# A gated cross-attention block on one core: the order of two tensor-engine tasks and the end of each step, first attention

## The chip, the core and the metric

The kernel runs on one core of a Trainium2 chip. The engines work in parallel, each through its own instruction queue in program order: PE (matrix products and transposes, into the eight banks of PSUM), ACT (activation functions and copies), DVE (vector operations, reductions), POOL (slow vector operations) and SP (issues the DMAs). They meet only at semaphores. The metric is the device time of one execution in microseconds (us).

## The reference, cut to what matters

Input `x` has 8 batches of 256 tokens with 256 features, the context has 77 tokens per batch. Four blocks follow each other, each added to `x` through a tanh gate:

1. cross-attention with 16 heads of 16 (this is the "first attention", and the only part that the change touches),
2. a sparse feed-forward block with three top-k choices,
3. a second cross-attention with rotary positions and a mask,
4. a mixture of 16 experts with a shared expert.

```python
q = split_heads(x0 @ Wq.T + bq)          # x0 = layernorm(x)
k = split_heads(ctx @ Wk.T + bk)
v = split_heads(ctx @ Wv.T + bv)
attn = softmax(-SCALE * einsum('bhqd,bhkd->bhqk', q, k))
out = einsum('bhqk,bhkd->bhqd', attn, v)
x = x + tanh(g) * (out @ Wp.T + bp)
x = x + tanh(g2) * ffn(layernorm(x))      # needs the second layernorm
```

## The kernel before, in words

The first attention works one batch of 256 queries per step n = 0 to 7. Batches are pipelined: in step n the kernel finishes the attention of batch n, prepares the queries and the softmax maxima of batch m = n + 2, transposes the normalised tokens of batch n + 3, projects the output of batch n - 1 and transposes the second-layernorm tokens of batch n - 2. The order on every engine is written out by hand: `attend` of PE (L1019), `attend` of ACT (L670), `attend_first` of DVE (L1570), `attend` of POOL (L514) and of SP (L380).

The tasks of PE in a step, with the short names used below:

- **KS01, KS23, KS45, KS67** (`key_scores`, L985): scores, keys by queries, of head pairs 0 to 7. Each pair goes to PSUM bank 0 or 1 in turn, so pair p waits until ACT has taken the exponential of pair p - 2 (`exp_done`).
- **PQ** (`project_q(m)`, L919): the query projection of batch m; waits for the copy of its transposed tokens (`xt_done`).
- **FR and SR** (`first_rows(m)`, `second_rows(m)`, L964 and L972): scores queries by keys for the first and second 128 queries of batch m, from which DVE takes the maximum over keys (`maxima`, L1531). Both use the same three banks, so SR waits for the maxima of FR. FR needs the rounded queries of ACT (`high_queries`, L621, "qhi").
- **W0 and W1** (`weigh_values(n, c)`, L1002): probabilities times values and the denominators, for heads 0 to 7 and 8 to 15; they wait for exponentials 3 and 7 of the batch.
- **PO** (`project_out(n-1)`, L935): the output projection; waits for the low part of the queries of m (`low_queries`, L1506, "qlo") because they share a bank.
- **MR** (`maxima_to_rows(m)`, L976): turns the maxima of batch m into rows; ACT copies them out (`maxima_out`, L643), and SP sends them through DRAM into the query operand of step m.
- **TX** (`transpose_xn(n+3)`, L911) and **TS** (`transpose_second(n-2)`, L915): four 128x128 transposes each; ACT copies them out with `copy_xt` (L609) and `round_xt` (L616).

Before the change a step of PE is KS01, PQ, KS23, FR, KS45, PO, SR, W0, KS67, TX, TS, MR, W1. In the steps 6 and 7 there is no batch m any more, and PQ, FR, SR and MR fall away; TX ends with step 4, and TS begins with step 2. All PE instructions of helper `mm` are recorded at L902, the transposes at L908.

ACT's step is: `invert(n-1, 1)` (L660: logarithm and exponential that make 1/denominator once W1 is done), exponentials 0 and 1, qhi, exponentials 2 to 5, `invert(n, 0)` once W0 is done, exponentials 6 and 7, `copy_xt`, `round_xt`, `maxima_out`. DVE's step is in the diff below, with `divide` (L1542) for the division, `add_projection` (L1493), the two parts of the second layernorm, and `low_part` (L1487), which waits for `round_xt`. POOL's step is `inv_std(n+4)` (L472: the 1/sigma that `normalise(n+4)` waits for), the block keys `kbr` of batch n + 3 (L489), the bias and the second 1/sigma. Before step 0 a prologue prepares the batches 0 and 1 completely; SP's `pair_maxima(1)` is its last DMA.

Of the kernel before, what the change touches and what calls it, by code (L numbers as in the profile page):

```python
# [50 lines left out]
def flamingo_kernel(nc, x_d, ctx_d, gates_d, mask_d, maskT_d, const_d,  # L51
                    ropeA_d, ropeB_d, attn_d, pat_d, piw_d,
                    pv_d, oiw_d, op_d, gate_d, wg_d, wu_d, wd_d, sg_d, su_d, sd_d, out_d):
    with ExitStack() as ctx:
# [549 lines left out]
        def _(act):  # L604
# [44 lines left out]
            def exponentials(n, pairs):  # L649
                for p in pairs:  # L650
                    act.wait_ge(score_ps, PAIRS * n + p + 1)
                    if n > 0:
                        act.wait_ge(pv_ps, 2 * n - 1 + p // 4)
                    if n == 0 and p == 0:
                        act.wait_ge(kone_in, 64)
                    act.activation(PT[n // B][0:SK, 2 * p:2 * p + 2, :],  # L656
                                   ps[0:SK, p % 2, :].rearrange("p (e q) -> p e q", e=2), ACT.Exp,
                                   scale=-0.25 if n < B else 1.0).then_inc(exp_done, 1)
# [11 lines left out]
            def attend(layer):  # L670
                lo, hi = B * layer, B * layer + B
                for n in range(lo, hi):
                    if n > lo:
                        invert(n - 1, 1)
                    exponentials(n, (0, 1))
                    if n == 2 * B - 1:
                        round_shared(0)
                    if n + 2 < hi:
                        if layer == 0:
                            high_queries(n + 2)  # L680
                        else:
                            raw_queries(n + 2)
                    exponentials(n, (2, 3, 4, 5))
                    if n == 2 * B - 1:
                        round_shared(1)
                    if n + 2 < hi and layer == 1:
                        high_queries(n + 2)
                    invert(n, 0)
                    exponentials(n, (6, 7))
                    if n + 3 < hi:  # L690
                        copy_xt(n + 3)
                    if n - 2 >= lo and layer == 0:
                        round_xt(n - 2, R_BANK + 1)
                    if n + 2 < hi:
                        maxima_out(n + 2)
                    if n == 2 * B - 1:
                        round_shared(2)
# [202 lines left out]
        def _(pe):  # L900
# [28 lines left out]
            def swap_pairs(m):  # L929
                pe.wait_ge(q_raw, m - B + 1)  # L930
                for g in range(2):
                    ins = mm(ps[:, m_bank(m), S * g:S * g + S], perm, qraw[:, g, :])
                ins.then_inc(q_perm, 1)
# [30 lines left out]
            def first_rows(m):  # L964
                pe.wait_ge(qhi_done, 2 * m + 2)
                pe.wait_ge(kbr_done, m + 1)
                if m > 0:
                    pe.wait_ge(max_done, 2 * m)
                pe.wait_ge(xt_done, m + 1)
                row_scores(m, 0)  # L970

            def second_rows(m):  # L972
                pe.wait_ge(max_done, 2 * m + 1)
                row_scores(m, 1)

            def maxima_to_rows(m):  # L976
                pe.wait_ge(max_done, 2 * m + 2)
                pe.wait_ge(qlo_done, m + 1)
                if m % B >= 3:
                    pe.wait_ge(x_done, m - 2)  # L980
                for t in range(2):
                    ins = mm(ps[0:H, m_bank(m), P * t:P * t + P], mcol[m % 2][:, t, :], ident_r)
                ins.then_inc(mT_ps, 1)

            def key_scores(n, pairs):  # L985
                for p in pairs:
                    if p == 0:
                        pe.wait_ge(k_in[n % 2], 32 * (n // 2 + 1))
                        pe.wait_ge(q_in[n % 2], 16 * (n // 2 + 1))
                        pe.wait_ge(m_in[n % 2], 16 * (n // 2 + 1))  # L990
                    if PAIRS * n + p > 1:
                        pe.wait_ge(exp_done, PAIRS * n + p - 1)
                    out = ps[0:SK, p % 2, :]
                    if n >= B:
                        mm(out.rearrange("p (e q) -> p e q", e=2), ident_b[:, 0:SK],
                           maskTb.unsqueeze(1).to_broadcast([P, 2, S]), True, False)
                    for e in range(2):
                        ins = mm(out[:, S * e:S * e + S], kpair[n % 2][0:KROWS, e, p, :], qpair[n % 2][0:KROWS, p, :],
                                 n < B, True)
                    ins.then_inc(score_ps, 1)  # L1000
# [18 lines left out]
            def attend(layer):  # L1019
                lo, hi = B * layer, B * layer + B  # L1020
                for n in range(lo, hi):
                    m = n + 2
                    key_scores(n, (0, 1))
                    if m < hi:
                        project_q(m)
                    key_scores(n, (2, 3))
                    if m < hi:
                        if layer == 0:
                            if m >= 5:
                                pe.wait_ge(xlo_done, m - 4)  # L1030
                            first_rows(m)
                        else:
                            swap_pairs(m)
                    key_scores(n, (4, 5))
                    if n > lo:
                        project_out(n - 1)
                    if m < hi:
                        if layer == 0:
                            second_rows(m)
                        else:  # L1040
                            first_rows(m)
                    weigh_values(n, 0)
                    if m < hi and layer == 1:
                        second_rows(m)
                    key_scores(n, (6, 7))
                    if n + 3 < hi:
                        pe.wait_ge(max_done, 2 * n + 6)
                        transpose_xn(n + 3)
                    if n - 2 >= lo and layer == 0:
                        if m < hi:  # L1050
                            pe.wait_ge(max_done, 2 * n + 6)
                        else:
                            pe.wait_ge(xlo_done, n - 2)
                        transpose_second(n - 2, R_BANK + 1, xn2[:, n % 2])
                    if m < hi:
                        maxima_to_rows(m)
                    weigh_values(n, 1)

            def project_keys(layer, j):
                g, nh = divmod(j, 2)  # L1060
# [371 lines left out]
        def _(dve):  # L1432
# [98 lines left out]
            def maxima(m, t):  # L1531
                dve.wait_ge(row_ps, 2 * m + t + 1)
                if m >= 2:
                    dve.wait_ge(mT_ps, m - 1)
                op = ALU.min if m < B else ALU.max
                heads = mcol[m % 2][:, t, :].rearrange("p (g h) -> p g h", g=2)
                dve.tensor_reduce(heads[:, :, 0:6], ps[:, R_BANK:R_BANK + 2, 0:6 * SK].rearrange("p g (h k) -> p g h k", k=SK),  # L1537
                                  AX, op, negate=True)
                dve.tensor_reduce(heads[:, :, 6:8], ps[:, R_BANK + 2, 0:4 * SK].rearrange("p (g h k) -> p g h k", g=2, k=SK),  # L1539
                                  AX, op, negate=True).then_inc(max_done, 1)  # L1540
# [29 lines left out]
            def attend_first():  # L1570
                for n in range(B):
                    if n > 0:
                        divide(n - 1, 1)
                    if n + 4 < B:
                        stats(n + 4)
                    if n + 2 < B:
                        low_queries(n + 2)
                    if n + 2 < B:
                        maxima(n + 2, 0)
                    if n + 4 < B:  # L1580
                        normalise(n + 4)
                    if n > 0:
                        add_projection(n - 1)
                    if n + 2 < B:
                        maxima(n + 2, 1)
                    if n > 0:
                        stats_second(n - 1)
                    if n == B - 1:
                        dve.wait_ge(kbr_done, B)
                        dve.wait_ge(xt_ps, B)  # L1590
                        for s in range(2):
                            split_patterns(0, s, None)
                    divide(n, 0)
                    if n > 0:
                        normalise_second(n - 1)
                    if n >= 2:
                        low_part(n - 2, R_BANK + 1)
# [454 lines left out]
```

## Time and profile before

| what | us |
|---|---|
| median of 3 runs | 807.88 (806.72 to 808.96) |
| profiled execution, its own time | 805.65 |
| its span in the trace | 803.8 |
| PE busy in the span | 693.6 (86%) |
| DVE, ACT, POOL busy | 453.2, 334.9, 219.9 |

The page of the profile gives the busy time of each engine, and the chain that ended last (73% of it on PE, 13% on DVE, 5% on ACT). The first attention with its steps 0 to 7 lies between about 35 and 148 us of the span. To read it, take the timeline of one step, put every row to its task by its operands (`ps<-keep,att` is PQ, `ps<-att,big` PO, `ps<-kbr,qhi` FR or SR, `ps<-qpair,kpair` key scores, `ps<-big,vp` the start of W0 or W1), and ask at each start what ended last before it. Starts are compared with starts: the rows of consecutive matmuls overlap.

### The profile page before, as it was taken

To read this page: it belongs to the slowest core of one execution; us is meant where nothing else is said; L and a number is where in the kernel's file an instruction comes from. 1 tells how busy PE (TensorE), PEld (TensorE's weight loads), DVE (VectorE), ACT (ScalarE), POOL (GpSimd) and SP (SyncE) were. 2 spreads that over 40 slices of the span, in tenths; PEclk is the share of its full clock that TensorE was granted. 3 is DMA by queue.
4 is the path that set the end of the run, shared out by engine and by line. 5 is a ranking of instruction groups with operands and counts; after the bars stand their busy time and mean duration, and the time that the engine had idled before them with its cause. 6 is when DMAs were issued, how large, how long until landed. Compare 5 with 4: busy or idle time off the path is not lost.

```text
span 803.8 us, 13689 instructions
## 1 busy us (share of the span) xinstructions
PE 693.6 (86%) x5104; PEld 556.7 (69%) x5104; DVE 453.2 (56%) x919; ACT 334.9 (42%) x757; POOL 219.9 (27%) x200
## 2 busy tenths in 40 slices
PE   5789998989996745766799998899988899999998
PEld 4556665668884423444566665699976799999997
DVE  4447773411006565747566563655878778788712
ACT  3245655556661110021355446423227655655510
POOL 6433421100000310024535521100005544554400
PEclk9869998999998865997899999999999999999999
DMA  6664672192000053004353342400000356566313
GB/s 241 179 169 134 173 207 74 66 403 84 11 0 2 1 199 96 8 0 123 88 134 94 98 127 54 154 5 1 1 1 1 108 198 219 193 195 233 127 37 105
DMA packets 61478, 87.22 MB, mean 109 GB/s; under 512 B 17264, under 2 KB 50800, under 8 KB 60400
## 3 DMA queue, kind: packets, MB, share of 16 engines
q1 hardware_dynamic: 61424, 86.49, 33.9%
q8 instruction: 35, 0.57, 0.3%
q14 instruction: 19, 0.16, 0.1%
HBM read 63.54 MB, written 18.73 MB: 102 GB/s over the span
## 4 chain that ended last, share of the span: by engine, by line
PE 73%; DVE 13%; issue 5%; ACT 5%; DMA 4%; SPq 1%; POOL 0%; ACTq 0%; DVEq 0%; POOLq 0%
PE ps L902 70%; DVE keep L1719 2%; PE ps L908 1%; DVE keep L1730 1%; ACT big L656 1%; DMA keep<-in_gates 1%; ACT keep L666 1%; DMA keep<-in_x 1%; DVE keep L1712 1%; DVE keep L1727 1%; PE ps L1379 1%; DMA k_rows<-klo 1%; DMA m_rows<-big 1%; DVE mcol L1539 1%; DVE mcol L1537 1%
## 5 line engine op out<-in xcount | busy, mean ns | idle before, releaser
L902 PE MATMUL ps<-keep 128*128 128x120 bf16 (+9 forms) x517 | 83.5, 286 | 38.7 <-DVE keep L1719 30.7
L902 PEld LDWEIGHTS ps<-keep 128*128 128x128 bf16 (+2 forms) x517 | 42.2, 119 | 65.7 <-DVE keep L1719 43.7
L902 PE MATMUL ps<-thi,whi 128*128 128x256 f32 x256 | 73.7, 288 | 4.3 <-POOL tlo L591 2.1
L902 PE MATMUL ps<-thi,wlo 128*128 128x256 f32 x256 | 72.4, 283 | 0.0
L902 PE MATMUL ps<-tlo,whi 128*128 128x256 f32 x256 | 72.4, 283 | 0.0
L745 ACT ACTIVATE ps<-ps 128x256 f32<-128x256 f32 x128 | 47.6, 372 | 38.6 <-PE ps L902 38.6
L902 PE MATMUL ps<-qpair,kpair 98*77 98x256 f32 x256 | 60.7, 355 | 3.3 <-ACT big L656 2.0
L495 POOL TENSOR_TENSOR kbr<-khi,keep 128x616 fp32r<-128x616 f32 x32 | 41.4, 1316 | 63.4 <-PE ps L902 63.4
L815 ACT ACTIVATE att<-ps 128x512 f32<-128x512 f32 x48 | 28.6, 596 | 68.6 <-PE ps L902 68.0
L902 PEld LDWEIGHTS ps<-thi,whi 128*128 128x128 f32 x256 | 49.0, 191 | 6.3 <-issue 4.1
L902 PE MATMUL ps<-xhi,phi 128*128 128x512 f32 x128 | 50.7, 396 | 2.9 <-ACT ps L745 2.9
L902 PE MATMUL ps<-big,vp 77*32 77x256 f32 (+1 forms) x384 | 46.8, 404 | 4.2 <-ACT big L656 3.9
L902 PE MATMUL ps<-xhi,plo 128*128 128x512 f32 x128 | 50.3, 393 | 0.0
L902 PE MATMUL ps<-xlo,phi 128*128 128x512 f32 x128 | 50.1, 392 | 0.0
L902 PEld LDWEIGHTS ps<-qpair,kpair 98*77 98x77 f32 x256 | 35.8, 157 | 20.0 <-issue 9.2
L902 PEld LDWEIGHTS ps<-tlo,whi 128*128 128x128 f32 x256 | 49.1, 192 | 0.0
L902 PEld LDWEIGHTS ps<-thi,wlo 128*128 128x128 f32 x256 | 49.0, 192 | 0.0
L666 ACT ACTIVATE keep<-ps,keep 128x256 f32<-128x256 f32 x32 | 15.2, 475 | 78.9 <-PE ps L902 78.9
L1855 DVE TENSOR_TENSOR att<-att,ps 128x512 f32<-128x512 f32 x48 | 32.7, 681 | 26.3 <-ACT att L815 23.5
L902 PE MATMUL ps<-kbr,qhi 128*128 128x154 f32 (+1 forms) x128 | 37.5, 404 | 9.7 <-DVE mcol L1539 4.1
L902 PE MATMUL ps<-big,keep 77*32 77x256 f32 (+3 forms) x480 | 40.8, 422 | 3.4 <-DVE keep L1809 1.0
L902 PE MATMUL ps<-keep,att 128*128 128x256 f32 x128 | 37.1, 442 | 4.5 <-ACT keep L613 4.5
(219 smaller groups left out, 1813.1 us busy)
## 6 DMA issues: line engine op xcount, KB each, us to landing
qpair<-q_rows SPq DMA_DIRECT2D x16, 768.0 KB, 5.6
q_rows<-qhi SPq DMA_DIRECT2D x32, 256.0 KB, 2.7
big<-in_piw SPq DMA_DIRECT2D x4, 2048.0 KB, 12.4
q_rows<-qlo SPq DMA_DIRECT2D x16, 256.0 KB, 2.9
att<-in_wg SPq DMA_DIRECT2D x8, 512.0 KB, 3.7
att<-in_wu SPq DMA_DIRECT2D x8, 512.0 KB, 4.7
att<-in_wd SPq DMA_DIRECT2D x8, 512.0 KB, 5.4
big<-in_wg SPq DMA_DIRECT2D x8, 512.0 KB, 3.6
```

The costliest lines, as they stand in the source:

```text
L495: ins = pool.tensor_tensor(kbr[n % 2][:, g], words(khi)[:, g, SK * b:SK * b + SK].unsqueeze(1).to_broadcast([P, HG, SK]), hmask.unsqueeze( ...
L656: act.activation(PT[n // B][0:SK, 2 * p:2 * p + 2, :], ps[0:SK, p % 2, :].rearrange("p (e q) -> p e q", e=2), ACT.Exp, scale=-0.25 if n < ...
L666: act.activation(r, ps[:, PV_BANK + c, S:2 * S], ACT.Ln, bias=tiny[:, 0:1]).then_inc(ln_done, 1)
L745: ins = act.activation(part, part, ACT.Gelu, accum_out=acts[:, bass.ds(ch * 8 + (2 * g + h), 1)])
L815: act.activation(hgl[:, f, :], ps[:, 2 * f, :], ACT.Gelu).then_inc(gelu_done, 1)
L902: return pe.matmul(out, lhsT, rhs, start=start, stop=stop, skip_group_check=True)
L908: ins = pe.transpose(ps[:, bank, at:at + P], src[:, t, P * c:P * c + P], ident)
L1379: ins = pe.transpose(ps[:, c_at + g // 2, at:at + P], GW[b % 2][:, t, P * g:P * g + P], ident)
L1537: dve.tensor_reduce(heads[:, :, 0:6], ps[:, R_BANK:R_BANK + 2, 0:6 * SK].rearrange("p g (h k) -> p g h k", k=SK), AX, op, negate=True)
L1539: dve.tensor_reduce(heads[:, :, 6:8], ps[:, R_BANK + 2, 0:4 * SK].rearrange("p (g h k) -> p g h k", g=2, k=SK), AX, op, negate=True).then_ ...
L1719: dve.tensor_tensor(reached[:, lo:hi, 8:P].rearrange("p c (j b) -> p c j b", b=8), chunked(keys)[:, lo:hi, :].unsqueeze(2) .to_broadcast([ ...
L1855: dve.tensor_tensor(hval, hgl[:, f, :], ps[:, 2 * f + 1, :], ALU.mult).then_inc(hval_done, 1)
```

## The change

For the first attention alone (layer 0): on PE, FR goes from between KS23 and KS45 to behind PO, and SR from in front of W0 to behind it; W1 goes from the end of the step to directly behind KS67; MR follows W1 and stands ahead of TX and TS. On ACT, `maxima_out` goes ahead of `copy_xt` and `round_xt`. On DVE, the first maxima go behind `normalise(n+4)` and `add_projection(n-1)`, and the second behind `divide(n, 0)`. So PE's new step is KS01, PQ, KS23, KS45, PO, FR, W0, SR, KS67, W1, MR, TX, TS. No instruction is added or removed; the second attention keeps its order.

```diff
--- before.py
+++ after.py
@@ -687,11 +687,13 @@
                         high_queries(n + 2)
                     invert(n, 0)
                     exponentials(n, (6, 7))
+                    if n + 2 < hi and layer == 0:
+                        maxima_out(n + 2)
                     if n + 3 < hi:
                         copy_xt(n + 3)
                     if n - 2 >= lo and layer == 0:
                         round_xt(n - 2, R_BANK + 1)
-                    if n + 2 < hi:
+                    if n + 2 < hi and layer == 1:
                         maxima_out(n + 2)
                     if n == 2 * B - 1:
                         round_shared(2)
@@ -1024,25 +1026,23 @@
                     if m < hi:
                         project_q(m)
                     key_scores(n, (2, 3))
-                    if m < hi:
-                        if layer == 0:
-                            if m >= 5:
-                                pe.wait_ge(xlo_done, m - 4)
-                            first_rows(m)
-                        else:
-                            swap_pairs(m)
+                    if m < hi and layer == 1:
+                        swap_pairs(m)
                     key_scores(n, (4, 5))
                     if n > lo:
                         project_out(n - 1)
                     if m < hi:
-                        if layer == 0:
-                            second_rows(m)
-                        else:
-                            first_rows(m)
+                        if layer == 0 and m >= 5:
+                            pe.wait_ge(xlo_done, m - 4)
+                        first_rows(m)
                     weigh_values(n, 0)
-                    if m < hi and layer == 1:
+                    if m < hi:
                         second_rows(m)
                     key_scores(n, (6, 7))
+                    if layer == 0:
+                        weigh_values(n, 1)
+                        if m < hi:
+                            maxima_to_rows(m)
                     if n + 3 < hi:
                         pe.wait_ge(max_done, 2 * n + 6)
                         transpose_xn(n + 3)
@@ -1052,9 +1052,10 @@
                         else:
                             pe.wait_ge(xlo_done, n - 2)
                         transpose_second(n - 2, R_BANK + 1, xn2[:, n % 2])
-                    if m < hi:
-                        maxima_to_rows(m)
-                    weigh_values(n, 1)
+                    if layer == 1:
+                        if m < hi:
+                            maxima_to_rows(m)
+                        weigh_values(n, 1)
 
             def project_keys(layer, j):
                 g, nh = divmod(j, 2)
@@ -1575,14 +1576,12 @@
                         stats(n + 4)
                     if n + 2 < B:
                         low_queries(n + 2)
-                    if n + 2 < B:
-                        maxima(n + 2, 0)
                     if n + 4 < B:
                         normalise(n + 4)
                     if n > 0:
                         add_projection(n - 1)
                     if n + 2 < B:
-                        maxima(n + 2, 1)
+                        maxima(n + 2, 0)
                     if n > 0:
                         stats_second(n - 1)
                     if n == B - 1:
@@ -1591,6 +1590,8 @@
                         for s in range(2):
                             split_patterns(0, s, None)
                     divide(n, 0)
+                    if n + 2 < B:
+                        maxima(n + 2, 1)
                     if n > 0:
                         normalise_second(n - 1)
                     if n >= 2:
```

## Rows read from the trace of the kernel before

**Rows 1.** The chain that ended last, shares by line, first attention (43 to 148 us).

```profile
by line: PE ps L902 75.6%; ACT big L656 8.3%; issue 7.8%; ACT keep L666 4.6%; ACT qhi L628 1.0%; PE ps L908 0.8%; ACT keep L668 0.6%; DVE mcol L1539 0.5%; DVE qlo L1510 0.5%; DVE big L1546 0.4%; ACTq L653 0.2%; ACTq L626 0.1%; ACTq L612 0.1
```

**Rows 2.** Busy time by stretch: us, then PE, PEld, DVE, ACT, POOL, clock, DMA share, GB/s.

```profile
80.00:92.90 12.90, 12.13 (x117) 8.91 (x116) 10.22 (x28) 7.78 (x18) 5.38 (x7) 1.00 0.67 188
...
118.90:131.30 12.40, 10.41 (x92) 6.50 (x92) 5.12 (x14) 6.80 (x15) 2.85 (x5) 0.86 0.58 162
```

**Rows 3.** The chain that ended last in order of time: start, us, what.

```profile
93.54 4.76 PE ps L902 x48
...
98.30 0.59 issue
...
106.47 4.75 PE ps L902 x48
```

**Rows 4.** Timeline from W1 of batch 3 to W1 of batch 4: start, us, what.

```profile
93.38 0.59 ACT L613 ACTIVATE keep<-ps 128x512 f32<-128x512 f32 x1
...
93.86 0.59 ACT L618 ACTIVATE xhi<-ps 128x512 fp32r<-128x512 f32 x1
...
94.34 0.36 ACT L647 ACTIVATE big<-ps 16x256 f32<-16x256 f32 x1
...
95.40 0.70 PE L902 MATMUL ps<-qpair,kpair 98*77 98x256 f32 x4
...
95.54 0.47 ACT L666 ACTIVATE keep<-ps,keep 128x256 f32<-128x256 f32 x1 [0.85 <-PE ps L902]
...
96.37 1.06 ACT L656 ACTIVATE big<-ps 77x512 f32<-77x512 f32 x2
...
97.48 0.82 PE L902 MATMUL ps<-qpair,kpair 98*77 98x256 f32 x4
...
97.95 0.84 ACT L628 ACTIVATE qhi<-ps,att 128x256 fp32r<-128x256 f32 x2 [0.52 <-PE ps L902]
...
98.68 1.07 ACT L656 ACTIVATE big<-ps 77x512 f32<-77x512 f32 x2
...
99.57 0.69 PE L902 MATMUL ps<-qpair,kpair 98*77 98x256 f32 x4
...
100.10 1.89 PE L902 MATMUL ps<-att,big 128*128 128x256 f32 x8
...
102.53 1.07 PE L902 MATMUL ps<-big,vp 77*32 77x256 f32 x16
...
104.53 0.47 ACT L666 ACTIVATE keep<-ps,keep 128x256 f32<-128x256 f32 x1 [3.45 <-PE ps L902]
...
104.93 0.60 PE L908 MATMUL ps<-keep 128*128 128x128 f32 x4
...
105.36 1.06 ACT L656 ACTIVATE big<-ps 77x512 f32<-77x512 f32 x2
...
105.36 0.60 PE L908 MATMUL ps<-keep,big 128*128 128x128 f32 x4
...
105.72 0.36 PE L902 MATMUL ps<-ident_r,mcol 128*16 128x128 f32 x2
```

**Rows 5.** Timeline: POOL's block keys and DVE's second normalisation side by side.

```profile
94.31 2.46 POOL L495 TENSOR_TENSOR kbr<-khi,keep 128x616 fp32r<-128x616 f32 x2
...
94.38 2.54 DVE L1484 TENSOR_SCALAR big<-keep 128x256 f32<-128x256 f32 x2 [0.76 <-POOL keep L487]
```

**Rows 6.** The large reduction of the maxima: name, count, ns min/median/max, starts.

```profile
L1537 DVE TENSOR_REDUCE mcol<-ps x32: 1085/1120/1121, 23.3 to 481.3; 128x12 fp32r<-128x924 f32 x32
```

**Rows 7.** Timeline of batches 0 and 1.

```profile
44.50 1.03 PE L902 MATMUL ps<-kbr,qhi 128*128 128x462 f32 x4 [1.77 <-DVE mcol L1539]
...
50.07 0.23 SPq L364 DMA_DIRECT2D qpair<-m_rows  x1
...
54.73 1.14 PE L902 MATMUL ps<-qpair,kpair 98*77 98x256 f32 x4
```

**Rows 8.** Busy time by stretch, one microsecond of W1 to projection of batch 1.

```profile
54.00:55.00 1.00, 1.00 (x9) 0.27 (x2) 0.00 (x0) 0.13 (x1) 0.00 (x0) 0.50 0.63 134
```

## The prediction

> **What bounds the kernel now.** Four views in this order. The chain by line, cut to the first attention, says who ends last there: PE for three quarters, then ACT with exponentials (L656) and the inversions (L666), and 7.8% "issue" [rows 1]. So this stage is a PE queue with ACT links in it. The busy time by stretch says how tight: 12.13 of 12.90 us in a full step, 10.41 of 12.40 in step 6, at a mean clock of 0.86 [rows 2]. PE can give back at most some 0.8 us per full step. The chain in time gives the period: W1 of batch 3 starts at 93.54, that of batch 4 at 106.47, so 12.93 us; inside is one stop of 0.59, where FR waits for qhi [rows 3]. The timeline of that step gives the distances that the new order has to be laid out with [rows 4]; zero is the start of W1(n), 93.54:
>
> - KS01 at +1.86 (so W1, and W0 too, holds PE 1.86); ACT's inversion at +2.00, after 0.85 idle; exponential 0 0.83 behind it, at +2.83.
> - qhi at +4.41, just when PQ ends; exponential 2 at +5.14, 3 done at +6.21.
> - PO at +6.56, W0 2.43 later (8.99), its inversion 2.00 behind W0, exponentials 6 and 7 from 2.83 to 3.90, W1 again at +12.93.
> - TX to TS 0.43, TS to MR 0.36, both behind KS67, while ACT inverts and takes exponentials 6 and 7 [rows 4]. PE would have to wait for exponential 7 anyway: this work is covered and costs nothing now. Likewise `copy_xt`, `round_xt`, `maxima_out` (0.48 from start to start, the last 0.36 long) lie on ACT under W1, where it has nothing else to do.
>
> **The change part by part.**
>
> *1. TX, TS and MR behind W1.* The cover is gone on PE: between W1 and the next KS01 and PQ now lie MR (two products; between 0.1 and 0.36, I take 0.25, somewhat under its row), TX 0.43 and TS 0.36: together 1.04. PQ ends at 4.41 + 1.04 = 5.45.
>
> *2. ACT's three copies.* They now wait for PE: `maxima_out` from +2.22 (1.86 + 0.36), `copy_xt` when TX is done, 1.86 + 0.25 + 0.60 = +2.71, `round_xt` behind it at +3.19, or with TS's end at 3.14. Queued behind them on ACT are the inversion of W1, exponentials 0 and 1 and qhi, which KS23, FR and all of DVE's query work wait for. The inversion starts at +3.67 and not +2.00, exponential 0 at 4.50, exponential 1 ends at 5.57. qhi starts at about 5.47: both roads, PE's and ACT's, arrive together, 1.06 late. Between the ends "ACT alone is late" (1.67, less the 0.5 it was early at qhi) and "PE alone" (1.04) hardly anything is open.
>
> *3. FR away from in front of KS45.* The 0.59 wait goes, but what is late next stands right behind: KS45 needs exponentials 2 and 3, which come behind qhi on ACT. They end at 5.47 + 0.73 + 1.07 = 7.27. So PE, free after KS23 at about 5.9, waits for them about 1.3 us in two pieces where it waited 0.59 and worked on FR. PO starts 0.35 behind exponential 3 (as now: 99.75 to 100.10), at 7.62: 1.06 late. Gain of this edit: none.
>
> *4. FR in SR's place, SR behind W0.* From PO to W0 one row-score task as before: 2.43, W0 at 10.05. Behind it PE has SR (about 0.6) and KS67. Pair 6 is scored 1.86 + 0.6 + 0.5 = 3.0 after W0, where the inversion lets ACT go on at 2.83: 0.15 lost. W1 starts at 10.05 + 3.0 + 1.07 + 0.04 = +14.16. The period is 14.16 against 12.93: **1.2 us more in each full step**. MR's maxima are no stop: SR's are done some 2 us after SR, W1 takes 1.86, and they must be ready only behind it.
>
> *5. DVE.* The first maxima now wait for `normalise(n+4)`, which falls together with POOL's block keys (both start when `inv_std` is done). DVE's two normalisations beside the block keys (two operations, 2.46) took 2.54 [rows 5], where others take 0.4 each. Unhindered, the maxima (1.12 and 0.47 [rows 6]) are ready before W0 ends; held up, they end about 0.3 late for SR. That is 0 to 0.6 per step in steps 2 and 3, the only full ones with a normalisation; I take 0.3. The Trainium skill, page "SBUF — State Buffer", section "SBUF: two separate sides", says that POOL and a DVE operation in a two-port mode exclude each other for a whole instruction, while operands in PSUM stay outside. By it the old order was a good cover (maxima read PSUM) and the new one a bad one; by the plain mean of the unhindered rows the 0.3 would be 0.
>
> *6. Step 0.* SR waits 1.77 us there for maxima and starts at 44.50; the clock then falls to 0.50 [rows 7, 8]. In the new order KS45, FR and W0 fill that time (to about 45.0), but the maxima come behind `normalise(4)` under the block keys: 2.4 later, so SR at 46.9, KS67, exponentials to 49.0, W1 at 49.05. At half clock W1 takes 3.7, MR and TX 1.4: KS01(1) at 54.15 against 54.73 [rows 7], a gain of 0.6. Bounds: if the clock holds, 51.6; but KS01(1) needs the maxima's DMA, issued at 50.07 [rows 7] and some 2 us on its way, so 52.1 at the best: 3 gained. The other way, 0.5 lost.
>
> *7. Steps 6, 7 and the way out.* No PQ, so ACT's late inversion counts in full. Behind W1(5): MR, TS, `maxima_out`, `round_xt` before the inversion, which starts 1.3 late; behind W1(6) and W1(7): TS and `round_xt`, 0.36 + 0.25 to its end + 0.48, about 1.0 late each, and the feed-forward block starts behind the last. Bounds 0.6 and 1.4 each.
>
> *8. SP.* `maxima_out` comes 1.5 to 2 us later, so `pair_maxima` too, with the queries of n + 3 behind it. The result is wanted a whole period later; I cost it nothing (0 to 0.2 a step).
>
> **The sum.** Step 0: -0.6. Step 2 (no TS before it): 1.1 + 0.3. Step 3: 1.2 + 0.3. Steps 4 and 5: 1.2 each. Then 1.3 + 1.0 + 1.0. Together +8.0. On the profiled execution's own 805.65 that is 813.65; the median of the runs shown is 2.2 above that execution, so the forecast is **815.9**.
>
> **The rivals.**
>
> *A, PE never waits (faster).* If KS45 found its exponentials ready and W1 its own, each full step would shrink to PE's work: 0.59 at FR and 0.15 to 0.8 in front of W1 go. Place: PE between KS23 and PO. Price: five stops of 0.59 and some 2 of the others, 5 us: 802.9. It decides at whether exponential 3 ends before PE comes to KS45's second pair; for it speaks the 1.77 of step 0, which does go. Against it: exponential 3 ended at 99.75 and FR, which filled that time, made way for KS45 at 99.57 [rows 4]; ACT can't be earlier than qhi, nor qhi than PQ.
>
> *B, the clock holds in step 0.* Clock 1.00 in place of 0.50 from 45 on: 3 us and not 0.6 gained, 813.5. Against it the new 1.9 us stop before SR.
>
> *C, the clock falls in the full steps.* Step 6 has 2.0 us without PE work and a mean clock of 0.86 [rows 2]; a new full step has 12.1 of work in 14.16, 2.0 idle as well, in two stops of about 1 us. Half clock over one output projection costs 1 to 1.7 us; in three or four steps +5: 821. Against it: the 2.0 are spread over a longer step with more products in it, and PQ and PO stand right beside the first stop.
>
> *D, the changes cancel (same).* Only if ACT's copies did not wait, and 1.04 of PE's were absorbed; 808.
>
> **How the numbers follow.** Forecast 0.55, C 0.18, B 0.12, A 0.10, D 0.05. A measurement of this kernel can tell about 0.3% (2.4 us) from no change. Slower: forecast, B and C, 0.85; same 0.05; faster A, 0.10. The range: the terms' bounds give 812 to 819.5 for the forecast; B and C widen it to 810 and 822; A and D stay outside.
>
> **What would show it.** In the changed kernel W1 starts about 14.1 us apart in steps 2 to 5. ACT's L666 behind W1 starts 3.7 us after it, with `maxima_out`, `copy_xt` and `round_xt` right before. KS45 is released by ACT L656, and PE is idle there for over 1 us; again about 1 us before W1. `first_rows` shows no wait of its own. The feed-forward block starts some 8 us later, and everything behind is only shifted. I'm wrong if the period is below 12.9 (ACT's exponentials earlier than I have them), if the half clock from 45 to 58 is gone, or if the steps 6 and 7 don't lengthen.

## The result, and the profile after

The changed kernel is slower: 820.67 us (median of 6 runs, 814.95 to 823.88) against 807.3 for the kernel before (6 runs, 805.17 to 810.43); ratio 1.016, 95% interval 1.0113 to 1.0207. That is 13.4 us more. The forecast was 8 us more (815.9, range 810 to 822). The profiled execution took 819.44 us with a span of 817.7, 13.9 more than the span before. 8.5 us of that lie in the first attention, where the change is, and 5.4 us behind it.

The chain of the changed kernel by line, over 43 to 165 us; its counterpart is [rows 1]:

```profile
by line: PE ps L904 68.2%; ACT big L656 11.3%; issue 8.2%; PE ps L910 3.5%; ACT keep L666 2.9%; ACT keep L613 1.6%; ACT xhi L618 1.5%; ACT qhi L628 1.4%; ACT keep L668 0.5%; DVE qlo L1511 0.5%; DVE big L1547 0.4%; ACTq L653 0.2%; ACTq L646 
```

ACT's exponentials (L656) have gone from 8.3% to 11.3%, and two lines are new in it: `copy_xt` (L613) and `round_xt` (L618), which had hung under W1 before. The same chain in order of time (start, us, what), from W1 of batch 3 to W1 of batch 4, as in [rows 3]:

```profile
96.44 2.16 PE ps L904 x34
...
99.08 0.46 ACT keep L613
...
99.58 0.59 ACT xhi L618
...
102.58 0.60 ACT big L656
...
110.57 2.16 PE ps L904 x34
```

The period is 14.13 us (96.44 to 110.57), where it was 12.93. The timeline of that step, to be laid beside [rows 4]:

```profile
98.31 0.30 PE L904 MATMUL ps<-ident_r,mcol 128*16 128x128 f32 x2
...
98.44 0.60 PE L910 MATMUL ps<-keep 128*128 128x128 f32 x4
...
98.64 0.37 ACT L647 ACTIVATE big<-ps 16x256 f32<-16x256 f32 x1 [2.25 <-PE ps L904]
...
98.88 0.60 PE L910 MATMUL ps<-keep,big 128*128 128x128 f32 x4
...
99.08 0.60 ACT L613 ACTIVATE keep<-ps 128x512 f32<-128x512 f32 x1
...
99.24 0.71 PE L904 MATMUL ps<-qpair,kpair 98*77 98x256 f32 x4
99.58 0.59 ACT L618 ACTIVATE xhi<-ps 128x512 fp32r<-128x512 f32 x1
...
99.79 1.94 PE L904 MATMUL ps<-keep,att 128*128 128x256 f32 x8
100.05 0.48 ACT L666 ACTIVATE keep<-ps,keep 128x256 f32<-128x256 f32 x1
...
101.85 0.84 ACT L628 ACTIVATE qhi<-ps,att 128x256 fp32r<-128x256 f32 x2
...
102.58 2.22 ACT L656 ACTIVATE big<-ps 77x512 f32<-77x512 f32 x4
...
103.22 0.95 PE L904 MATMUL ps<-qpair,kpair 98*77 98x256 f32 x4 [0.76 <-ACT big L656]
...
103.70 0.21 PEld L904 LDWEIGHTS ps<-qpair,kpair 98*77 98x77 f32 x2 [0.27 <-ACT big L656]
...
104.00 1.89 PE L904 MATMUL ps<-att,big 128*128 128x256 f32 x8
...
106.43 1.07 PE L904 MATMUL ps<-big,vp 77*32 77x256 f32 x16
...
110.57 0.64 PE L904 MATMUL ps<-big,vp 77*32 77x256 f32 x8 [0.93 <-ACT big L656]
```

Read from W1 at 96.44: MR, TX and TS at +1.87, +2.00 and +2.44; KS01 at +2.80 (before +1.86); `copy_xt` ends at +3.24 and PQ starts at +3.35 (before +2.40). ACT inverts at +3.61 (before +2.00), qhi starts at +5.41 (+4.41), the first pair of KS45 waits 0.76 for exponential 2 (the bracket names the idle time and its releaser; the row holds both pairs, and the second, whose weights load at 103.70, follows exponential 3 with no such stop), PO is at +7.56 (+6.56), W0 at +9.99 (+8.99), and W1 itself waits 0.93 for exponential 7. So the step is 1.0 us late from PQ on, and 0.2 more behind W0.

The whole first attention by the starts of W1 in the two timelines, in us:

```
            W1(0)  W1(1)  W1(2)  W1(3)  W1(4)   W1(5)   W1(6)   W1(7)   first pattern product
before      51.16  67.70  80.62  93.54  106.47  119.40  131.78  144.63  149.71
after       50.46  68.22  82.33  96.44  110.57  124.69  138.46  152.12  158.25
difference  -0.70  +0.52  +1.71  +2.90  +4.10   +5.29   +6.68   +7.49   +8.54
```

Behind it the difference grows in one part only. The stretch from the end of the pattern products to the first exponential of the second attention, and the rest (us; busy time of PE, PEld, DVE, ACT, POOL; granted clock; DMA share; GB/s), before and after:

```profile
242.15:385.15 143.00, 88.67 (x727) 58.00 (x725) 91.95 (x259) 20.10 (x44) 27.31 (x33) 0.78 0.21 65
385.15:801.00 415.85, 390.47 (x3037) 339.36 (x3036) 263.36 (x425) 188.55 (x309) 136.11 (x92) 0.99 0.32 103
```

```profile
250.69:399.09 148.40, 94.77 (x727) 62.32 (x725) 91.99 (x259) 20.21 (x45) 27.29 (x33) 0.73 0.20 63
399.09:815.00 415.91, 390.44 (x3037) 339.42 (x3036) 263.08 (x425) 188.51 (x309) 135.85 (x92) 0.99 0.32 103
```

148.40 against 143.00 us for the same instructions, at a mean clock of 0.73 against 0.78; the remaining 415.9 us are equal. This stretch (top-k, then the prologue of the second attention) has PE at work in short pieces between waits, and PE's busy time in it goes from 88.67 to 94.77 us. DVE's, ACT's and POOL's hardly move. An estimate from the two granted clocks, since every row here is at 0.50 or at 1.00: about 63 us of this stretch ran at half clock before, and about 80 after.

### The profile page after: what moved, and what is told of

It is laid out like the page before. It is cut to its first block, busy times and chain, and to the rows that moved or that the text cites. A ratio compares the mean times of both kernels' runs of the same rounds, so it can differ in the third digit from the quotient of the medians.

```text
span 817.7 us, 13689 instructions
## 1 busy us (share of the span) xinstructions
PE 702.0 (86%) x5104; PEld 561.5 (69%) x5104; DVE 452.5 (55%) x919; ACT 336.1 (41%) x757; POOL 220.0 (27%) x200
## 4 chain that ended last, share of the span: by engine, by line
PE 73%; DVE 12%; ACT 6%; issue 5%; DMA 3%; SPq 1%; POOL 0%; ACTq 0%; DVEq 0%; POOLq 0%
PE ps L904 70%; DVE keep L1720 2%; ACT big L656 2%; PE ps L910 2%; DVE keep L1731 1%; DMA keep<-in_gates 1%; DVE keep L1713 1%; DVE keep L1728 1%; ACT keep L666 1%; DMA k_rows<-klo 1%; DMA m_rows<-big 1%; DVE mcol L1538 1%; DVE mcol L1540 1%; PE ps L1380 1%; DVE att L1856 1%
## 5 line engine op out<-in xcount | busy, mean ns | idle before, releaser
L904 PE MATMUL ps<-keep 128*128 128x120 bf16 (+9 forms) x517 | 85.4, 292 | 38.2 <-DVE keep L1720 30.4
L904 PEld LDWEIGHTS ps<-keep 128*128 128x128 bf16 (+2 forms) x517 | 43.9, 122 | 65.5 <-DVE keep L1720 43.3
L904 PE MATMUL ps<-qpair,kpair 98*77 98x256 f32 x256 | 62.5, 358 | 9.6 <-ACT big L656 8.4
L904 PE MATMUL ps<-big,keep 77*32 77x256 f32 (+3 forms) x480 | 42.6, 439 | 3.4 <-DVE keep L1759 1.0
L904 PEld LDWEIGHTS ps<-big,vp 77*32 77x32 f32 (+1 forms) x384 | 31.2, 140 | 18.0 <-ACT big L656 10.3
L904 PE MATMUL ps<-keep,att 128*128 128x256 f32 x128 | 39.4, 462 | 4.5 <-ACT keep L613 4.5
```

What stands on the lines that cost most here:

```text
L904: return pe.matmul(out, lhsT, rhs, start=start, stop=stop, skip_group_check=True)
```

## The experiments

Names of tasks as above. In the tables "period" is the distance of W1 in the full steps, taken from each kernel's profile; the totals are medians, and "slower" is against the kernel before, run beside each. The diffs are cut to the lines that carry the edit: conditions that only keep the second attention as it was, and in 1, 2, 4 and 5 the parts on ACT and DVE that the text names, are left out.

**1. The end of the step alone.** W1, MR, TX, TS and `maxima_out` first, as in the changed kernel; FR, SR and DVE as before.

```diff
 key_scores(n, (6, 7))
+if layer == 0:
+    weigh_values(n, 1)
+    if m < hi:
+        maxima_to_rows(m)
 if n + 3 < hi:
...
-if m < hi:
-    maxima_to_rows(m)
-weigh_values(n, 1)
```

> The end of the step alone: in the first attention W1, MR, TX, TS on PE and maxima_out first on ACT, as in the changed kernel; FR, SR and DVE's order as before. Theory 1 (the end of the step is the price, the row scores are worth nothing): the period of W1 in steps 2 to 5 is 14.0 us (PQ 1.04 later, qhi 1.06 later, then as before), steps 6 and 7 as long as in the changed kernel (13.7), the way out 1 us longer; the step 0 loses about 1 us more than the changed kernel, since the wait for the maxima stays. In all 8 to 10 us over the kernel before. Theory 2 (FR and SR are what costs, because KS45 now waits for the exponentials): the period stays near 12.9 and the whole within 2 us of the kernel before.

Measured: 837.65 us (6 runs), ratio 1.0391 (1.0356 to 1.0425), 31 us slower; periods 15.11, then 17.1 in every step from 3 to 7. Neither theory said so. Timeline: W1 of the steps 2 and 3; then the busy time by stretch between them:

```profile
83.76 1.92 PE L904 MATMUL ps<-big,vp 77*32 77x256 f32 x16 [1.39 <-ACT big L656]
...
100.89 0.66 PE L904 MATMUL ps<-big,vp 77*32 77x256 f32 x4 [1.39 <-ACT big L656]
```

```profile
91.00:100.50 9.50, 7.91 (x66) 5.88 (x64) 8.34 (x22) 5.24 (x12) 4.48 (x5) 1.00 0.42 145
101.00:107.50 6.50, 6.50 (x47) 4.32 (x48) 2.80 (x3) 1.86 (x4) 4.38 (x4) 0.50 0.66 151
```

W1 waits 1.39 us for exponential 7, and right behind it the clock goes from 1.00 to 0.50 for over 6 us, in each step. W1, MR, TX, TS, KS01 and PQ then run at 1.2 GHz in place of 2.4.

**2. The row scores alone.** FR behind PO, SR behind W0, DVE's two maxima behind `add_projection`; the end of the step as before.

```diff
-    second_rows(m)
 weigh_values(n, 0)
+    second_rows(m)
 key_scores(n, (6, 7))
 if n + 3 < hi:
     pe.wait_ge(max_done, 2 * n + 6)   # TX waits for SR's maxima
```

> The row scores alone: FR behind PO, SR behind W0, on DVE both maxima behind the added projection and ahead of the second statistics; the end of the step as before (TX, TS, MR, W1; copy_xt, round_xt, maxima_out). Theory 1: PO is no later than before (6.56 after W1), W0 neither; SR behind W0 and the maxima behind SR make TX and W1 0.2 to 0.5 later, so a period of 13.1 to 13.4; steps 6 and 7 as before; step 0 gains 0.7 to 1.5. In all 0 to 2 us over the kernel before. Theory 2: the period is 14 us and the whole 6 us or more slower.

Measured: 812.05 us, ratio 1.0093 (1.0058 to 1.0128), 5.6 us slower; period 14.45. From W1 to W0 the step is as long as before (8.97 against 8.99), as theory 1 had it, but W0 to W1 takes 5.48 and not 3.94. The numbers are nearer to theory 2 (14 us, 6 or more), but not for its reason. The timeline shows what stands between:

```profile
93.73 0.87 PE L902 MATMUL ps<-kbr,qhi 128*128 128x462 f32 x4
...
94.64 1.12 DVE L1531 TENSOR_REDUCE mcol<-ps 128x12 fp32r<-128x924 f32 x1 [1.10 <-PE ps L902]
...
95.67 0.47 DVE L1533 TENSOR_REDUCE mcol<-ps 128x4 fp32r<-128x308 f32 x1
...
96.20 0.66 PE L908 MATMUL ps<-keep 128*128 128x128 f32 x4 [1.12 <-DVE mcol L1533]
```

SR at 93.73, its maxima from 94.64 to 96.14, and TX, which overwrites a bank that the maxima read, stands 1.12 us for them. I had put that at 0.2 to 0.5. The cover is the point: with SR behind W0, TX and MR can't run in front of W1 any more without this stop. So the two halves of the change belong together: each alone has a stop that the changed kernel doesn't have or has shorter (1.12 us before TX here, 1.39 before W1 in experiment 1 against 0.93).

**3. ACT's inversion ahead of the three copies** (changed kernel otherwise).

```diff
 exponentials(n, (6, 7))
+if layer == 0:
+    invert(n, 1)
 maxima_out / copy_xt / round_xt
```

> The changed kernel, but on ACT the inversion for W1 of step n stands ahead of maxima_out, copy_xt and round_xt, so it does not wait for MR, TX and TS. Theory 1 (in full steps PE's 1.04 and ACT's queue arrive together): exponential 0 starts 0.3 us earlier, qhi at the same time, period 14.1 still, at most 0.1 less; steps 6 and 7 and the way out, where ACT is alone, 0.5 us shorter each: 1.5 us less than the changed kernel. Rival (ACT's late inversion is the price in full steps too): the period falls to 13.1 to 13.6, and 5 us come back.

Measured: 816.86 us, ratio 1.0143 (1.0103 to 1.0183); period 14.54 in the full steps, longer than 14.12. The rival is out, and theory 1 missed the period too. The total is 3.8 us below the changed kernel's although the first attention is longer in the profile, by 2.4 us: the stretch behind it took 142.52 here and not 148.40 (experiment 8). The intervals of the two ratios overlap. The gains that theory 1 saw behind step 5 didn't come: step 7 and the way out were 1.2 and 1.8 us longer than in the changed kernel, at granted clocks of 0.66 and 0.62 against 0.88 and 1.00. Timeline (W1 is at 94.90):

```profile
96.90 0.47 ACT L666 ACTIVATE keep<-ps,keep 128x256 f32<-128x256 f32 x1 [2.05 <-PE ps L905]
...
97.99 0.57 ACT L613 ACTIVATE keep<-ps 128x512 f32<-128x512 f32 x1
...
98.61 1.99 PE L905 MATMUL ps<-keep,att 128*128 128x256 f32 x8 [0.21 <-ACT keep L613]
```

The inversion is early (+2.00), but `copy_xt` now ends at +3.66, and PQ waits for it until +3.71 (changed kernel +3.35). In the changed kernel three roads end within about 0.1 us of each other: PE's own tasks, the copies that PQ waits for, and ACT's queue up to qhi.

**4. The changed kernel with TS in PE's stop.** TS (with `round_xt` and `low_part`) goes from behind MR into the stop between KS23 and KS45 of the next step.

```diff
 key_scores(n, (2, 3))
+if layer == 0 and n >= 3:
+    pe.wait_ge(max_done, min(2 * n + 4, 2 * B))
+    transpose_second(n - 3, R_BANK + 1, xn2[:, (n - 3) % 2])
 key_scores(n, (4, 5))
```

> The changed kernel with TS of batch n-3 (ACT's round_xt and DVE's low part with it) taken from the end of step n-1 into PE's 1 us stop between KS23 and KS45 of step n. Theory 1 (what stands behind W1 is on the path, what stands in the stop is not): PQ 0.36 earlier, the inversion 0.48 earlier, qhi 0.4 earlier, period of the steps 3 to 5 about 13.7 in place of 14.1, step 6 0.7 and step 7 1.0 shorter, the way out 1.0 shorter; 3.5 to 4.5 us less up to the feed-forward block. Rival (the path runs through the row scores and maxima): the period stays 14.1.

Measured: 813.41 us (7 runs), ratio 1.0096 (1.0063 to 1.0129), 7.6 us slower than before, so nearly half of the loss is back; but the period stays 14.11 in three of the four full steps (14.64 in the fourth). The period is the rival's, but the path doesn't run through the row scores, as the rival had it. The pattern products start at 155.47 in place of 158.25. Of these 2.8 us, 1.2 are there at W1(1) already (67.02 against 68.22), where both kernels run the same code; that is how far two executions lie apart. The rest comes in the steps 6 and 7 and the way out, less 0.5 lost in step 3. The stretch behind the pattern products takes 143.0 and not 148.4 (experiment 8 is on that). Timeline (W1 at 109.88):

```profile
112.52 0.60 ACT L613 ACTIVATE keep<-ps 128x512 f32<-128x512 f32 x1
...
113.17 1.99 PE L906 MATMUL ps<-keep,att 128*128 128x256 f32 x8 [0.22 <-ACT keep L613]
...
116.65 0.95 PE L906 MATMUL ps<-qpair,kpair 98*77 98x256 f32 x4 [0.58 <-ACT big L656]
```

PQ waits 0.22 for `copy_xt` and starts at +3.29: in the changed kernel TS had run under this copy. I had put TS on the path; what is on it are MR, TX and the copy.

**5. Experiment 4, and in addition TX ahead of MR, and `copy_xt` ahead of `maxima_out`.**

```diff
 weigh_values(n, 1)
-maxima_to_rows(m)
 transpose_xn(n + 3)
+maxima_to_rows(m)
```

> The kernel with TS in the stop before KS45, and in addition TX ahead of MR on PE and copy_xt ahead of maxima_out on ACT. In the former the period had stayed at 14.11, against my 13.7, and PQ had waited 0.22 for copy_xt. Theory 1a (PQ waits for the later of two roads: PE through MR, TX, TS and KS01, and MR, TX and ACT's copy of 0.6; taking TS away freed only the first): now both are shorter, PQ starts 3.1 to 3.2 after W1 and not 3.29, and the period is 13.9 to 14.0. Rival: the period stays at 14.11, and something else holds it.

Measured: 817.67 us (4 runs), ratio 1.0121 (1.007 to 1.0171); period 14.36 in three of the four full steps (14.81 in the other), longer than either theory had it. Timeline (W1 at 96.22):

```profile
98.78 0.60 ACT L613 ACTIVATE keep<-ps 128x512 f32<-128x512 f32 x1 [2.61 <-PE ps L910]
99.27 0.36 ACT L647 ACTIVATE big<-ps 16x256 f32<-16x256 f32 x1
...
99.77 1.97 PE L904 MATMUL ps<-keep,att 128*128 128x256 f32 x8 [0.43 <-ACT big L647]
```

The bracket of PQ names the other copy: `project_q` also waits for `maxima_out` (`mT_done`), since MR and PQ use one bank. So PQ stands behind both of ACT's copies, in whatever order, and the changed order is the better of the two.

**6. The end of the step alone, with PE's stop filled.** Six products of 128x256 ahead of W1 in the steps 0 to 5.

```diff
 if m < hi:
+    pe.wait_ge(max_done, 2 * m + 2)
+    for j in range(6):
+        mm(ps[:, R_BANK + 2, 0:S], wq[:, 0, 0:P], xnT_b[:, 0, :])
 weigh_values(n, 1)
```

> The kernel with the end of the step alone, plus six products of 128x256 in front of each W1 of the steps 0 to 5 (their result is overwritten), which fill PE's wait for exponential 7. Its unfilled form had a period of 17.1 us where my walk gave 14.0, and its clock stood at 0.50 for over 6 us of each step. Theory 1 (the 3 us are the half clock, which PE's two stops let in): with the stop filled the clock stays at 1.00 and the period falls to 14.0 to 14.4. Rival (a dependency that I overlooked makes 17.1): it stays at 17 or rises.

Measured: 829.19 us (4 runs), ratio 1.0302 (1.0248 to 1.0357); 8.5 less than unfilled, with more work in it. Busy time by stretch over the steps 2 to 5, and the filling in one of them:

```profile
65.61:126.63 61.02, 58.86 (x501) 43.50 (x500) 39.31 (x89) 30.99 (x67) 18.81 (x23) 1.00 0.59 161
```

```profile
108.89 2.75 PE L904 MATMUL ps<-keep,att 128*128 128x256 f32 x12
...
109.33 1.06 ACT L656 ACTIVATE big<-ps 77x512 f32<-77x512 f32 x2
...
111.57 1.07 PE L904 MATMUL ps<-big,vp 77*32 77x256 f32 x16
```

The clock stays at 1.00 for all 61 us, and the period falls to 15.05 to 15.7. It isn't 14.0 because each of the six is two matmul instructions: they end 1.1 us after exponential 7 (110.39). Less that, 15.06 - 1.14 = 13.9, about my walk without a clock (14.0). So of the 3 us per step of experiment 1, 2 are measured as gone, and the third is worked out by this subtraction; they were the half clock. That the stop let it in is shown in this one place.

**7. Step 0 alone, on the kernel before.** W0 ahead of SR in step 0.

```diff
-second_rows(m)
+if n > 0:
+    second_rows(m)
 weigh_values(n, 0)
+if n == 0:
+    second_rows(m)
```

> The kernel before with one move in step 0 alone: W0 stands ahead of SR there, so PE works on it where it waited 1.77 us for the maxima. Theory 1 (the only wait that the change really removed): W1(0) starts 1 to 3 us earlier, KS01(1) no earlier than about 52.1 (the DMA of the maxima), so at most 2.6 us of the first attention are gained, periods of steps 2 to 5 stay 12.93; the whole 0 to 3 us faster, unless the part behind the first attention changes with the start. Rival: the clock falls to half in step 0 all the same and nothing is gained (within 0.5 us).

Measured: 804.59 us (12 runs, 799.85 to 808.26) against 805.79 for the kernel before, ratio 0.9982 (0.9951 to 1.0012): faster than the changed kernel, and not told apart from the one before. In the profile the first attention is 2.9 us shorter (146.79 against 149.71), and KS01(1) stands near the bound of the forecast (52.1), 0.6 earlier:

```profile
41.54 1.07 PE L902 MATMUL ps<-big,vp 77*32 77x256 f32 x16
...
43.77 0.87 PE L902 MATMUL ps<-kbr,qhi 128*128 128x462 f32 x4 [0.29 <-DVE mcol L1540]
...
51.53 1.11 PE L902 MATMUL ps<-qpair,kpair 98*77 98x256 f32 x4 [0.61 <-DMA qpair<-m_rows]
```

W0 runs at 41.54, SR waits 0.29 and not 1.77, and KS01 of batch 1 now waits for the DMA of the maxima. The clock fell later, too: its mean from 40 to 58 us is 0.81 here, 0.59 in the kernel before and 0.50 in the changed one. The 2.9 us are the wait and the clock together, and nothing here parts them.

**8. A plain delay in front of the feed-forward block**, to ask for the 5.4 us behind the first attention: the kernel before with 40, then with 48 products that nothing uses.

```diff
 pe.wait_ge(xlo_done, 6)
+pe.wait_ge(pat_split, 1)
+for j in range(40):              # 48 in the second, 11 in the third
+    mm(ps[:, 3, :], phi[:, 0, 0:P], xhi[:, 0, 0:512])
```

> The kernel before with 40 extra products of 128x512 (into a bank that is overwritten afterwards) on PE between the first attention and the feed-forward block: 40 x 0.217 = 8.7 us of delay, nothing else changed. It asks whether the 5.4 us by which the profiled changed kernel is longer behind the first attention come from starting 8.5 us later. Theory 1 (chance of where the half-clock stretches fall in an execution): the median rises by 8.7 us, within 1.5. Rival (everything behind is longer whenever it starts later by this much): it rises by 12 to 14.

> The kernel before with 48 extra products in place of 40 between the first attention and the feed-forward block: 10.4 us of delay where 40 gave a median 13.4 us longer. Theory 1 (what lies behind takes more or less time by where its half-clock stretches fall, and this depends on the start, not only on chance of a run; the profile with a start 11 us late had lost nothing behind it): the whole is 10.5 to 11.5 us longer, less than with 40. Rival (every later start costs more behind it): 14 us or more.

Measured: 819.87 us with 40 (5 runs, ratio 1.0168, 1.0133 to 1.0203): 13.4 us for a delay of 9.4 in the profile. That is the rival's number. 818.11 with 48 (5 runs, ratio 1.0167, 1.0126 to 1.0209): 12.3 us by the medians for a delay of 11.2, between the two theories. The stretch that took 143.00 and 148.40 above, with 40 and with 48:

```profile
251.31:398.99 147.68, 93.90 (x727) 61.48 (x725) 92.00 (x259) 20.19 (x45) 27.29 (x33) 0.74 0.20 63
```

```profile
252.97:395.48 142.51, 87.34 (x727) 57.08 (x725) 92.00 (x259) 20.10 (x45) 27.31 (x33) 0.79 0.21 65
```

A third, 11 products in the changed kernel:

> The changed kernel plus 11 extra products (2.4 us) on PE between the first attention and the feed-forward block. In the profiles so far the part from the end of the pattern products to the first exponential of the second attention took 148.4 and 147.7 us where it began at 250.7 and 251.3, but 142.5 where it began at 253.0 and 253.1, and 143.0 at 242 to 248.5. Theory 1 (about 5 us of the measured 13 are this, and depend on the start alone): with 2.4 us of delay it begins at 253.1 and takes 142.5, so the kernel with more work is 2 to 4 us faster than the changed one, about 817. Rival (chance of the runs): it is 2.4 us slower, 823.

Measured: 820.73 us (6 runs, 815.56 to 824.01; ratio 1.0155, 1.0113 to 1.0198), where the changed kernel had 820.67: the 2.4 us of work cost nothing that can be seen, but didn't give the gain of theory 1 (817) either. The aim was missed: in its profile the stretch began at 254.80, not at 253.1, and took 146.33. Its first attention, the same code as the changed kernel's, had come out 1.3 us later (pattern products from 159.51 against 158.25).

All profiles, one per kernel, by where this stretch began. The row "median" comes from the medians of all runs: by how much the kernel is slower than the one before, less by how much its stretch began later in the profile:

```
began at  239.19  242.15  247.88  248.50  249.21  250.69  251.31  252.97  253.10  254.80  261.34  271.69
took      143.29  143.00  143.02  143.04  147.95  148.40  147.68  142.51  142.52  146.33  145.20  145.52
median    +1.8    0       +1.9    -0.8    +3.9    +4.8    +4.2    +1.5    -0.6    +1.3    +4.2    +1.6
kernel    exp 7   before  exp 4   exp 2   exp 5   after   40      48      exp 3   11      exp 6   exp 1
```

The first attention has no part in these numbers: a kernel whose first attention is untouched shows the same 5 us when its start is 9 us late, and 1.7 us later they are gone. The granted clock is 0.73 and 0.74 in the three long ones and 0.77 to 0.79 in the others. The medians go the same way (+3.9 to +4.8 where the stretch was long, at most +1.9 elsewhere except in experiment 6), so the long form isn't a chance of the one execution that was profiled. That the start decides it is the reading that fits best, but it is not shown: the one run that was to forecast it missed its start, and runs of one kernel differ by 9 to 11 us among themselves (815 to 824 changed, 800.6 to 811.2 before).

## Why the prediction was right, point by point

The time lies in the range, but not in the bounds that the forecast's own terms gave (812 to 819.5). It is inside only because rival C, which did not happen where it was placed, had widened the range to 822. That part is luck.

- **Parts 1 and 2, the end of the step: right in size, wrong in one member.** The lateness at qhi was forecast as 1.06 and measured as 1.00 (+5.41 against +4.41). But the sum "MR, TX and TS" of 1.04 was not what held PQ. Experiment 4 took TS away and the period stayed; experiment 5 showed the wait for both copies. The road is MR, TX, copy; the other two roads (PE's 0.94 to KS01, ACT's queue) are as long, which is why the number came out; to that extent it is luck.
- **Part 3, FR moved without gain: right in the balance.** The 0.59 wait went, KS45 waits in its place, PO is 1.00 late. The wait was forecast as about 1.3 in two pieces; it is 0.76, in front of the first pair, for exponential 2. Experiment 2 shows the same balance alone: FR moved, KS45 waiting, PO still 6.56 behind W1.
- **Part 4: right.** W1 to W0 9.99 (forecast 10.05), W0 to W1 4.14 (4.11), period 14.11 to 14.13 (14.16).
- **Part 5, DVE under POOL's block keys: the collision is there, its price not.** In step 0 it is exact:

```profile
42.70 2.46 POOL L495 TENSOR_TENSOR kbr<-khi,keep 128x616 fp32r<-128x616 f32 x2
42.77 2.54 DVE L1462 TENSOR_SCALAR keep<-keep 128x256 f32<-128x256 f32 x2
...
45.23 1.10 DVE L1538 TENSOR_REDUCE mcol<-ps 128x12 fp32r<-128x924 f32 x1
...
47.38 1.48 PE L904 MATMUL ps<-kbr,qhi 128*128 128x462 f32 x4
...
54.93 1.20 PE L904 MATMUL ps<-qpair,kpair 98*77 98x256 f32 x4
```

The first maxima wait for the normalisation and start at 45.23. In the steps 2 and 3 the normalisation took 1.9 and 2.4 and not 0.8, but ended about when the output projection did, for which DVE waits next anyway; the 0.3 per step was 0 (periods 14.11 in steps 2 and 3, 14.13 and 14.12 in steps 4 and 5, which have no normalisation). The Trainium skill (page "SBUF — State Buffer", section "SBUF: two separate sides") has it that one of the two blocks the other for whole instructions; the trace agrees, with 2.54 beside 2.46. That another wait can swallow it is what the forecast missed.
- **Part 6, step 0: the wait went, the gain didn't come.** SR at 47.38 (46.9), W1(0) at 50.46 (49.05), KS01(1) at 54.93 (54.15): a loss of 0.2 where I had a gain of 0.6, inside the bound of 0.5 lost. The clock stood at 0.50 from 40 to 58 in this profile, so W0, SR and KS67 too ran at half clock. The maxima were ready at 46.7, as forecast; what held SR until 47.38 was W0 at half clock, and not the maxima. W1, MR and TX then took 4.47 and not 5.1. Neither number is firm: in three executions of this same code W1(1) came at 67.02, 68.22 and 69.24, in three of the old code at 67.22, 67.43 and 67.70.
- **A term left out: step 1.** My sum went from step 0 to step 2. Step 1's period grew by 1.22 (17.76 against 16.54), of which 0.9 had been spent by KS01(1), inside part 6.
- **Part 7: right.** Steps 6 and 7 and the way out +1.39, +0.81, +1.05, against 1.3, 1.0, 1.0.
- **Part 8: right.** No key scores of the steps 1 to 7 wait for the maxima's DMA in the changed kernel.
- **The sum.** Up to the pattern products: forecast +8.0, measured +8.54. Steps 0 and 1 were 1.1 short, the full steps 0.5 too long.
- **The step that failed** is the one that ended the sum there: "everything behind is only shifted". It held for the last 415 us, but not for the 143 before them, which took 5.4 us more in the profile; with 8.5 they make the 13.9 of the span. The medians are 13.4 apart. My clock rival C looked for this only inside the full steps, at the right price and in the wrong place; there the clock held at 1.00. Experiment 1 shows how near that was: the same end of step without the row-score moves pays 3 us in each step.
- **Rival A** (PE never waits) is refuted by KS45's and W1's waits. **Rival B** failed in the changed kernel, but experiment 7 shows that the wait it rested on was real: with the clock that it kept, 2.9 us of the profile. **Rival D** (the changes cancel) is refuted by the ratio and by the copies, which did wait.

What stays open: why the half clock hits every step of experiment 1 from 3 on and no full step of the changed kernel, where PE stops twice as well (1.39 before W1 there, 0.93 here); and how often a run of the changed kernel falls in the long form of the stretch behind (its six runs spread over 8.9 us).

## What to carry to other kernels

Before a task is moved off the place where it fills another engine's latency, ask what fills that place next, and what becomes late at the new one; here TX, MR and three copies lay free under ACT's exponentials and W1, and behind W1 they cost 1.0 us a step. Lay out all roads to the next common point: three were about equally long, so shortening one (TS in experiment 4, ACT's queue in experiment 3) gave nothing in the period. And a local delay need not be passed on one to one where, as here, the granted clock changes and PE works in short pieces: measure the part behind it too, with a plain delay.

## What the runs showed that I had not expected

- A step order with a stop of 1.39 us before W1 had its clock at 0.50 for over 6 us in each of five steps, at a steady period of 17.1 us; with the stop filled by useless products the clock was 1.00 and the kernel 8.5 us faster.
- The same instructions took between 142.5 and 148.4 us in twelve profiles, and near starts gave near times across different kernels: 250.7 and 251.3 gave 148.4 and 147.7, 252.97 and 253.10 gave 142.51 and 142.52.
- 48 idle products cost less in the whole (12.3 us) than 40 (13.4 us), but the two intervals overlap, so this isn't told apart from no difference.
